# Keys contracted in 64-row halves of one image instead of from a stacked copy

## What is computed

```python
# layer 1: linear attention, 8 heads of 32
xn  = (x - mean_c(x)) / sqrt(var_c(x) + 1e-5) * g + b      # over the 64 channels
q, k, v = split(einsum('bchw,oc->bohw', xn, w_qkv))        # 3 x 256 rows
q = q * 32**-0.5
k = softmax(k, over the 1024 positions)
context = einsum('bhcn,bhdn->bhcd', k, v)
out = einsum('bhcd,bhcn->bhdn', context, q)                # then w_out, + b_out, + xn
# layer 2: binary convolution
y  = conv3x3(sign(x1), sign(W));  yn = batchnorm(y) * gamma + beta
result = yn + x1
```

## Time and profile before

| | |
|---|---|
| median of 3 runs | 99.69 us (99.69 to 99.94) |
| span of the profiled execution | 98.3 us |
| time of a run outside the span (99.69 less 98.3) | 1.4 us |
| PE busy | 81.6 us, 83% |
| DVE busy | 62.3 us, 63% |
| ACT busy | 56.7 us, 58% |
| POOL busy | 41.6 us, 42% |
| granted TensorE clock, mean | 0.952 of full |
| DMA | 8.89 MB, mean 90 GB/s |

### The profile page before, as it was taken

The page is one execution under the profiler, slowest core; times in us unless marked ns, Lnnn a source line. Parts: engine busy times, 40 slices in busy tenths (PEclk is TensorE's granted clock), DMA queues, the critical chain, the costliest instruction groups (busy, mean ns, idle before and its releaser), DMA issues.

```text
span 98.3 us, 2063 instructions
## 1 busy us (share of the span) xinstructions
PE 81.6 (83%) x771; PEld 47.5 (48%) x771; DVE 62.3 (63%) x119; ACT 56.7 (58%) x110; POOL 41.6 (42%) x55
## 2 busy tenths in 40 slices
PE   4999988999999999999999999999999999100000
PEld 4923423368575457565756656767564545100000
DVE  4826787967399509546885599539717297669600
ACT  2225957788898477087691745868313296189000
POOL 6999281283295442071693391859100000006400
PEclk9999999999999999999999999999999999995555
DMA  1998013104200213000042000714400808105893
GB/s 46 306 352 311 7 53 105 53 9 122 86 3 0 68 51 100 1 0 0 0 136 81 0 0 0 168 52 83 130 7 0 198 22 183 30 0 148 257 322 127
DMA packets 4748, 8.89 MB, mean 90 GB/s; under 512 B 1430, under 2 KB 1746, under 8 KB 4740
## 3 DMA queue, kind: packets, MB, share of 16 engines
q1 hardware_dynamic: 3540, 7.46, 26.0%
q0 software_dynamic: 336, 1.05, 3.4%
q10 hardware_dynamic: 864, 0.26, 1.1%
HBM read 2.51 MB, written 2.10 MB: 47 GB/s over the span
## 4 chain that ended last, share of the span: by engine, by line
PE 70%; DVE 11%; ACT 7%; issue 4%; ACTq 1%; POOLq 1%; POOL 1%; DVEq 0%
PE ps L832 8%; PE ps L846 8%; PE ps L833 7%; PE ps L734 5%; PE ps L922 5%; PE ps L933 4%; PE ps L858 4%; PE ps L903 4%; PE ps L797 4%; DVE mx L573 4%; PE ps L973 3%; PE ps L878 3%; PE ps L885 3%; PE ps L864 2%; DVE XN L548 2%
## 5 line engine op out<-in xcount | busy, mean ns | idle before, releaser
L578 DVE TENSOR_REDUCE mxp<-ps 128x2 bf16<-128x1024 f32 x12 | 14.7, 1224 | 11.3 <-PE ps L797 11.3
L423 ACT ACTIVATE E<-ps 128x512 f32<-128x512 f32 x32 | 17.8, 596 | 3.3 <-PE ps L833 3.2
L330 POOL TENSOR_TENSOR E_lo<-E 128x512 bf16<-128x512 f32 x11 | 12.5, 1162 | 7.2 <-ACT E L423 7.1
L832 PE MATMUL ps<-wk_max,S 128*128 128x256 bf16 x64 | 15.2, 275 | 0.0
L833 PE MATMUL ps<-wk_lo,S 128*128 128x256 bf16 x64 | 15.1, 272 | 0.0
L335 POOL DMA_DIRECT2D out<-OUT x3 | 1.8, 606 | 20.2 <-DVE OUT L724 20.2
L298 POOL TENSOR_TENSOR x_lo<-XN,x_hi 128x512 bf16<-128x512 f32 x8 | 9.2, 1155 | 2.5 <-DVE x_hi L554 2.4
L352 ACT ACTIVATE sq<-ps 128x512 f32<-128x512 f32 x8 | 4.8, 603 | 8.2 <-PE ps L734 8.2
L734 PE MATMUL ps<-X,center_mat 128*128 128x512 f32 x16 | 9.4, 693 | 0.0
L287 POOL CAST x_hi<-XN 128x512 bf16<-128x512 f32 x6 | 3.7, 612 | 13.4 <-DVE XN L548 13.4
L644 DVE SCALAR_TENSOR_TENSOR X<-XN,vec,ps 128x1024 f32<-128x1024 f32 (+1 forms) x5 | 5.2, 1066 | 5.4 <-PE ps L903 5.4
(11 more groups left out here) (137 smaller groups left out, 158.9 us busy)
## 6 DMA issues: line engine op xcount, KB each, us to landing
X<-in_x SPq DMA_DIRECT2D x3, 512.0 KB, 5.0
X<-X SPq DMA_DIRECT2D x4, 256.0 KB, 3.6
X<-X SPq DMA_DIRECT2D x8, 128.0 KB, 2.3
S<-x_hi SPq DMA_DIRECT2D x7, 126.0 KB
S<-x_lo SPq DMA_DIRECT2D x7, 126.0 KB
out<-OUT SPq DMA_DIRECT2D x3, 256.0 KB, 4.0
out<-OUT POOLq DMA_DIRECT2D x3, 256.0 KB, 4.5
X<-in_x SPq DMA_DIRECT2D x2, 256.0 KB, 3.7
```

The lines of the kernel that those rows point to most:

```text
L330: nc.gpsimd.tensor_tensor(e_lo, e, e_hi, ALU.subtract).then_inc(elo_pool, 1)
L423: nc.scalar.activation(E[:, b % 2, 2 * g:2 * g + 2, :].rearrange("p k j -> p (k j)"), kt_ps[g % 2], ACT.Exp).then_inc(exp_ready, 1)
L578: nc.vector.tensor_reduce(mxp[:, h, :, t], k_ps, AX.X, ALU.max).then_inc(max_ready, 1)
L832: nc.tensor.matmul(dst, chunk, wk_max[:, b % 2, :], start=True, stop=False)
```

## The change

A unit is now one whole image, with positions 0 to 511 on partitions 0 to 63 and 512 to 1023 on partitions 64 to 127. X, XN, x_hi and x_lo are [128, 8, 512].

- `keys_t(b, g)` reads x_hi and x_lo directly, not S. Each group covers both halves and both banks: per 128 positions of each half three matmuls with 64 rows (hi by wk_max, hi by wk_lo, lo by wk_hi), the halves alternating. There are two groups of 12 an image instead of four groups of four.
- wk_max is made for each image by DVE from PSUM (`shift_keys`), all 128 rows; the maximum is put in two columns of mx (`both_rows`), and `max_rows` makes a full 128-row product. ACT's `row` copies, `join_max` and POOL's constant rows and wk_max copies go. The constant rows are written with `split_hi`, by a multiply and an add per partition (hi_rows).
- Maxima come per image, `key_max(b, 0)` and `key_max(b, 1)`, each over 1024 positions.
- S is still stacked, now only for `apply_matrix`. XN is moved by 16 more DMAs into the old pair layout in X (`X_pairs`), and `add_input` works on it in place.
- fp32 variances: units 0 to 2 (before 0 to 4). Centering runs three images ahead.
- The queues of PE, ACT and DVE become one loop over images; wk_hi moves from ACT to DVE; `split_exp(b - 1)` stands in DVE's queue in image b, `apply_matrix(b - 6)` in images 6 and 7.

The core of the diff. Where a new loop or body replaces an old one written out line by line, only some of the removed lines are shown.

```diff
-            for q in range(1, PAIRS):
-                sp.dma_start(X[:, q, :], x_d[q]).then_inc(x_loaded[q + 1], 16)
+            for n, part in enumerate((slice(1, 2), slice(2, 4), slice(4, B)), 1):
+                for h in range(HALVES):
+                    sp.dma_start(X[half(h), part, :], x_h[h, :, part, :]).then_inc(x_loaded[n], 16)
...
+            for q in range(PAIRS):
+                pair = slice(2 * q, 2 * q + 2)
                 wait_hi(sp, 2 * q + 1)
+                if q == 0:
+                    wait_hi(sp, 0)
+                for h in range(HALVES):
+                    sp.dma_start(S[0:C, pair, h * BANK:(h + 1) * BANK], x_hi[half(h), pair, :]
+                                 ).then_inc(stacked[q], 16)
                 sp.wait_ge(lo_ready, 2 * q + 2)
+                for h in range(HALVES):
+                    sp.dma_start(S[C:P, pair, h * BANK:(h + 1) * BANK], x_lo[half(h), pair, :]
+                                 ).then_inc(stacked[q], 16)
+                sp.wait_ge(scaled, 2 * q + 2)
+                for d in two:
+                    for h in range(HALVES):
+                        sp.dma_start(X_pairs[half(d), q, h * BANK:(h + 1) * BANK], XN[half(h), 2 * q + d, :]
+                                     ).then_inc(xn_moved[q], 16)
...
-                nc.gpsimd.tensor_copy(x_hi[:, q, part], XN[:, q, part]).then_inc(hi_ready, 1)
+                if n == 1:
+                    pool.wait_ge(rows_ready, 6)
+                nc.gpsimd.tensor_scalar(x_hi[:, n, :], XN[:, n, :], hi_rows[:, 0:1], hi_rows[:, 1:2], ALU.mult, ALU.add
+                                        ).then_inc(hi_ready, 1)
...
             for b in range(B):
+                n = b + LN_AHEAD
                 exp(b, 0)
                 exp(b, 1)
+                if n < B:
+                    square(n)
+                if b == 0:
+                    query_value_weights()
+                if b + 1 < SPLIT:
+                    keep_xt(b + 1)
+                if b:
+                    keep_pt(b - 1)
+                if n < B:
+                    log_var(n)
+                    inverse_std(n)
+                exp(b, 2)
+                exp(b, 3)
+                if b == 0:
+                    out_weights()
                 if b == 4:
                     tap_signs()
+                if b == 5:
                     keep_taps()
...
+            def key_max(b, t):
+                dve.wait_ge(k_ready, NT * b + t + 1)
+                if b == 0 and t == 0:
+                    dve.wait_ge(mx_zeroed, 1)
+                if b >= 2 and t == 0:
+                    dve.wait_ge(row_done, b - 1)
+                nc.vector.tensor_reduce(mx[:, b % 2, t, 0:1], k_ps(b, t).rearrange("p a n -> p (a n)"), AX.X, ALU.max
                                         ).then_inc(max_ready, 1)
 
+            def both_rows(b):
+                dve.wait_ge(max_ready, NT * (b + 1))
+                nc.vector.tensor_copy(mx[:, b % 2, :, C:C + 1], mx[:, b % 2, :, 0:1]).then_inc(mx_ready, 1)
+
+            def shift_keys(b):
+                dve.wait_ge(row_done, b + 1)
+                nc.vector.tensor_tensor(wk_max[:, b % 2, :], row_ps, wk_hi[:], ALU.add).then_inc(row_ready, 1)
...
+            dve.wait_ge(wk_done, 1)
+            nc.vector.tensor_copy(wk_hi[:], w_ps[:, 0:HID]).then_inc(wkh_ready, 1)
             dve.wait_ge(wkh_ready, 1)
             nc.vector.tensor_tensor(wk_lo[:], w_ps[:, 0:HID], wk_hi[:], ALU.subtract).then_inc(wkl_ready, 1)
+            normalise(0)
+            dve.wait_ge(scaled, 1)
+            nc.vector.tensor_scalar(x_hi[:, 0, :], XN[:, 0, :], hi_rows[:, 0:1], hi_rows[:, 1:2], ALU.mult, ALU.add
+                                    ).then_inc(hi_first, 1)
...
+            normalise(1)
+            key_max(0, 0)
+            key_max(0, 1)
+            both_rows(0)
+            shift_keys(0)
             normalise(2)
...
                 dve.wait_ge(f_done, HALVES * q + end)
-                nc.vector.scalar_tensor_tensor(X[:, q, part], XN[:, q, part], vec[:, G_:G_ + 1], f_ps[q][:, part],
-                                               op0=ALU.mult, op1=ALU.add).then_inc(x1_ready, end - first)
+                dve.wait_ge(xn_moved[q], 16 * 2 * HALVES)
+                nc.vector.scalar_tensor_tensor(X_pairs[:, q, part], X_pairs[:, q, part], vec[:, G_:G_ + 1],
+                                               f_ps[q][:, part], op0=ALU.mult, op1=ALU.add
+                                               ).then_inc(x1_ready, end - first)
...
+            for b in range(B):
+                if b + 1 < B:
+                    key_max(b + 1, 0)
+                if b == 0:
+                    out_rows()
+                if SPLIT <= b + 1 < B:
+                    keep_xt(b + 1)
+                if b + 1 < B:
+                    key_max(b + 1, 1)
+                    both_rows(b + 1)
+                if b > SPLIT:
+                    split_exp(b - 1)
+                if b + 1 < B:
+                    shift_keys(b + 1)
+                if b + LN_AHEAD < B:
+                    normalise(b + LN_AHEAD)
+                if b in (3, 5, 7):
+                    split_m(b // 2 - 1)
+                if b and b < LAST:
+                    scale_r(b - 1)
+                if b >= 6:
+                    add_input(b - 6, 0, 2)
+
+            split_exp(LAST)
+            scale_r(LAST - 1)
             add_input(2, 0, 2)
+            scale_r(LAST)
...
             def keys_t(b, g):
                 if g == 0:
                     pe.wait_ge(row_ready, b + 1)
-                    pe.wait_ge(s_const, 4 if b < 2 else 8)
-                    if b:
-                        pe.wait_ge(stacked[b // 2], 64 if b > 1 else 32)
-                if b == 0 and g % 2 == 0:
-                    pe.wait_ge(stacked_first[g // 2], 32)
-                if b == 0 and g == 1:
-                    pe.wait_ge(lnv_ready, AHEAD)
-                if b * GROUPS + g >= 2:
-                    pe.wait_ge(exp_ready, b * GROUPS + g - 1)
+                    pe.wait_ge(lo_ready, b + 1)
+                if b or g:
+                    pe.wait_ge(exp_ready, b * GROUPS + HALVES * g)
                 for k in (2 * g, 2 * g + 1):
-                    dst = kt_ps[g % 2][:, (k % 2) * HID:(k % 2 + 1) * HID]
-                    chunk = S[:, b, k * P:(k + 1) * P]
-                    nc.tensor.matmul(dst, chunk, wk_max[:, b % 2, :], start=True, stop=False)
-                    last = nc.tensor.matmul(dst, chunk, wk_lo[:], start=False, stop=True)
-                last.then_inc(kt_ready, 1)
+                    chunk = slice(k * P, (k + 1) * P)
+                    dst = [kt_ps[h][:, (k % 2) * HID:(k % 2 + 1) * HID] for h in range(HALVES)]
+                    for h in range(HALVES):
+                        nc.tensor.matmul(dst[h], x_hi[half(h), b, chunk], wk_max[half(h), b % 2, :],
+                                         start=True, stop=False)
+                    for h in range(HALVES):
+                        nc.tensor.matmul(dst[h], x_hi[half(h), b, chunk], wk_lo[half(h), :], start=False, stop=False)
+                    for h in range(HALVES):
+                        last = nc.tensor.matmul(dst[h], x_lo[half(h), b, chunk], wk_hi[half(h), :],
+                                                start=False, stop=True)
+                        if k % 2:
+                            last.then_inc(kt_ready, 1)
 
...
                 pe.wait_ge(mm_ready, q + 1)
+                pe.wait_ge(stacked[q], 16 * 2 * HALVES)
...
             variance(0)
             pe.wait_ge(wtk_ready, 1)
             pe.wait_ge(tk_built, 1)
             nc.tensor.matmul(w_ps[:, 0:HID], t_keys[:].rearrange("c d s -> c (d s)"), w_t[:, 0:HID],
                              start=True, stop=True).then_inc(wk_done, 1)
+            variance(1)
             for j in range(2 * NT):
                 last = nc.tensor.transpose(o_ps[0:C, j * P:(j + 1) * P], w_in[:, (0, 1, 4, 5)[j], :], ident[:])
             last.then_inc(qvraw_done, 1)
+            center(2)
+            shift_maxima(0, 0)
+            shift_maxima(0, 1)
             variance(2)
             transpose_x(0)
             make_query_value_weights()
+            max_rows(0)
+
+            for b in range(B):
                 keys_t(b, 0)
+                if b in (3, 5, 7):
+                    matrix(b // 2 - 1)
+                if b + 1 < B:
+                    shift_maxima(b + 1, 0)
+                if b + LN_AHEAD < B:
+                    center(b + LN_AHEAD)
+                if b + 1 < B:
+                    transpose_x(b + 1)
+                    shift_maxima(b + 1, 1)
+                if b == 0:
+                    transpose_out_weights()
+                elif b <= SPLIT:
+                    context(b - 1)
+                else:
+                    split_context(b - 1)
+                if b + LN_AHEAD < B:
+                    variance(b + LN_AHEAD)
+                if b + 1 < B:
+                    max_rows(b + 1)
                 keys_t(b, 1)
```

(77 more changed lines are left out.)

390 lines of the change are left out of this document (91 added, 299 removed).

## The result

The changed kernel takes 114.8 us (median of 4 runs, 114.3 to 116.3) against 99.8: 1.149 times the kernel before, 95% interval 1.145 to 1.153. The forecast was 112.8 (106 to 120). The span of the profiled execution (114.77 us) is 112.6, which is 14.3 more; around it lie 2.2, where 1.4 was taken for the kernel before. That 1.4 joins a median with the span of another, longer execution: in every later execution on record, of every kernel tried, 2.0 to 2.3 lie around the span, and those of the kernel before with a span of 98.3 took 100.3 and 100.4. By this the profiled execution of the kernel before was some 0.6 longer than its median.

What follows compares the result with a forecast made beforehand. TensorE's queue bounds the kernel before; after the change PE waits on ACT and DVE queue order. Start -0.9, images 1 to 4 +3.8, images 5 to 7 +10.2: +13.1 on 99.7 gives 112.8 us, range 106 to 120.

Steps and rivals of the forecast that it cites:

- PE's work falls and does not set the time: PE's sum falls by 5.2 us, a key group of pairs taking 0.65, but waits made by the new queue order cost more.
- keys_t(b+1, 0) waits for the exponentials behind log_var and inverse_std: Images 1 to 4: PE waits 1.2 before each next keys, cycle 7.7 us; with image 3's matrix +3.8 in all.
- Image 3: The matrix at b=3 adds 0.75 to the 7.7 us cycle.
- Images 5 to 7: Waits on DVE's split_exp behind the maxima, then on ACT's signs: 9.2 + 8.45 + 8.1 = 25.75 against 15.5, +10.2.
- both_rows and split_exp together: On DVE behind the second maximum in images 5 and 6: both_rows 0.2, split_exp about 1.1.
- Image 7 and the convolution's wait of 2.7: Image 7 takes 8.1 us; PE waits 2.7 before the convolution, released by signs.
- The start: Keys of image 0 at 16.7 against 17.82, image 0 itself 8.7 against 8.6: net -0.9.
- The moves of XN at nothing: Sixteen added moves on SP's queue feed only readers images later: 0, at most 3.7 if one were late.
- From the convolution on unchanged: Behind the convolution's start the order is the old one on all engines, so no change in time.
- One of the forecast's own signs of being wrong: The forecast is wrong if the clock row shows 5 before the end.
- The rival was priced at +8: PE's clock falls to half in images 5 to 7: +8, 120.8 us; chance 0.11.
- The rival of serial pairs: Key pairs don't overlap at 256 columns: 1.3 more an image, 10.4 in all, 123 us; chance 0.04.
- the room left for the clock: The range's upper end of 120 reaches toward the clock case, 120.8, beyond the likeliest case's own 109 to 116.

Runs made afterwards that it cites:

- e10_one_half_again: Reordered kernel with all key matmuls on one partition half (second half's keys computed from the first's rows): 106.4 us, 7.5 more than the reordered kernel.
- reordered kernel: Changed kernel with new queue orders only, same instructions but for one E_lo that goes from POOL to DVE: 98.9 us, ratio 0.988 to the kernel before.
- e11_taps_between: Reordered kernel with transpose_taps moved between the high and low part of split_context(4): 98.93 us, ratio 0.989 to the kernel before.
- e9_keys_back: Reordered kernel, images 1 to 4: second keys again behind the context, log_var and inverse_std ahead of the last exponentials: 106.9 us.
- e2_split_first: Changed kernel with split_exp at the head of each image in DVE's queue instead of behind the two maxima: 114.4 us.
- e3_no_moves: Changed kernel without the sixteen DMAs that move XN; add_input adds the raw input instead: 118.3 us (114.2 to 119.7).
- e5_again: The changed kernel itself once more, unedited, on another chip than the first four experiments: 118.5 us (117.7 to 118.6).
- e1_keys_early: Changed kernel, images 0 to 6: second key group ahead of the context, its exponentials ahead of keep_pt, log_var and inverse_std: 117.0 us.
- e4_serial_halves: Changed kernel with the three key terms of one half issued in a row, then those of the other: 116.3 us, ratio 1.149 to the kernel before.
- e6_filled_gaps: Changed kernel with unread filler matmuls in PE's gaps of images 1 to 5 and ahead of the convolution, none in image 0: 117.4 us.

## Why the prediction was right

- *PE's work falls and does not set the time*: right. A key pair holds 0.11 (a group of six pairs holds 0.66, forecast 0.65), shown from the other side by `e10_one_half_again`: 0.93 an image, 7.5 in all. PE's busy time at full clock is 76.2 in the reordered kernel against 81.6, 5.4 less; busy time is not what the array is held, but the forecast of 5.2 less fits it. With the order mended the kernel is 1.2% faster than before (0.6 to 1.9), not 5.2 us: it reaches image 1's keys 3.4 us earlier, wins 0.5 in images 1 to 4, and gives 3.4 back in images 5 to 7 (18.9 against 15.5), where `e11_taps_between` shows DVE as the bound. At the convolution's start 0.5 is left; most of the other 1.0 between the two profiled spans lies behind the last store.
- *keys_t(b+1, 0) waits for the exponentials behind log_var and inverse_std*: right, 1.27 for 1.2, cycle 7.80 for 7.7 in images 1, 2 and 4. `e9_keys_back` shows that this order, with the place of the second keys, costs 7.7 in four images.
- *Image 3*: missed by 0.74. The price of `matrix` was right, but project(2) waits for split_m(0) behind normalise on DVE. The working followed DVE's maxima to 5.9 and not the small entries behind them. This is most of the 1.0 by which images 1 to 4 were under-forecast.
- *Images 5 to 7*: 25.5 for 25.75. The order of DVE's queue was right, and `e2_split_first` confirms its price by itself (-1.40, -1.23). One size was wrong, both_rows and split_exp together, taken as 1.3 from the earlier trace rows. In image 5 they took 1.43 (0.83 + 0.60, by the chain), with POOL at its own parts of E_lo until 65.04. In image 6 POOL had ended at 70.72 when they ran, and they took 0.77 (0.17 + 0.60): this is the 0.5 by which image 6 came out shorter.
- *Image 7 and the convolution's wait of 2.7*: right, 2.7.
- *The start*: right, 16.71 for 16.7. The moves of XN at nothing: right, by `e3_no_moves`.
- *From the convolution on unchanged*: wrong, +1.4 and -0.7, put at nothing because the order there is the old one. The wait of 2.7 was in the forecast and its effect on the clock only in a rival. One of the forecast's own signs of being wrong, a 5 in the clock row before the end, came in slice 31. The rival was priced at +8 for a clock low in all of images 5 to 7; what came was short, 1.4 in the first profile and 5.1 of the same kernel's 118.5 in `e5_again`. The Trainium skill, page "TensorE: Matmul & The Clock Gate", section "Why this matters for your kernels", warns of idle gaps between bursts. The traces agree so far, with 1.4 us lost behind a wait of 2.7 (and, in `e1_keys_early`, `center` at 2.00 for 1.05 behind one of 2.7), but the same wait of 2.7 brought no fall in `e2_split_first`, `e4_serial_halves` and `e5_again`.
- *The rival of serial pairs*: it did not come, a pair takes 0.11. One rule of the Trainium skill, page "TensorE: Matmul & The Clock Gate", Part 3, lets a weight load overlap a running matmul only in another row group. The trace disagrees: on one half the key matmuls of `e10_one_half_again` follow at 0.11 each (0.22 a pair), the pace of the keys in the kernel before, and their loads add nothing to it.
- *Luck and slips*: against the forecast, images 1 to 4 (+1.0), the convolution (+1.4) and what lies around the span (+0.8) came long, the start with image 0 (-0.2), images 5 to 7 (-0.2, with image 6's -0.5 in them) and the end (-0.7) short. So a part of the nearness of 112.8 to 114.8 is errors that cancel, and at 118.5, as in `e5_again`, the same kernel stays inside the range only through the room left for the clock. Three slips of the working: the context is added as 1.97 for its 1.88; the start with image 0 is -1.0 by its own numbers, not -0.9; and 98.3 and 1.4 are off from a median execution by about 0.7 each, one high and one low, which cancels in the sum.

What stays open: why the clock falls in image 0 or 4 in one execution and not in another, at the same gaps (the chips differ too, which no run separates). Image 0's 2.4 and the rest of the gain in images 5 to 7 were not tried one order at a time. The kernel before was not reordered, so what the new layout is worth against it at the best order of each is not shown.

## What to carry to other kernels

When a change makes the bounding engine's work smaller, ask what in the other engines' queues now stands ahead of the thing it needs next; here PE's busy time did fall by 5.4 us, and the queue orders cost 15.9 until they were rewritten. Follow each queue to its last small entry, not only through its large ones. A wait in the bounding engine can cost a second time, if its clock falls behind it, and time won in one place comes back as a wait where another engine's queue is full.

## What the runs showed of the hardware

- Matmuls on the two partition halves start side by side even when three of the first half stand ahead in the queue (`e4_serial_halves`, 43.29); in `e10_one_half_again` a maxima matmul of the other half (L734, 32.01) starts 0.10 before the key matmul queued ahead of it (L760, 32.11).
- The granted clock fell to half in stretches where PE had waited 0.9 to 2.7 us between bursts, for 3.4 us or more each time, at places that differ between executions of the same kernel: 114.8 and 118.5 us. The same waits stood elsewhere without a fall, and in `e9_keys_back` two waits of 0.6 to 1.3 in each of images 1 to 4 brought none. With fillers in the gaps it stayed up in the one execution profiled (`e6_filled_gaps`).
- DVE's E_lo of 128x512 took 0.68 in the mean of five in the changed kernel, and 1.08 in the mean before. Before, four of the five ran beside an E_lo of POOL and took 0.97 to 1.52, and the fifth, behind POOL's last, 0.68. In the changed kernel POOL was at work beside the first only, which took 0.68 all the same, behind a both_rows of 0.83 that takes 0.17 in image 6. So POOL beside it can double the time, and need not.
